# A Gram matrix from two fp16 words per value, and the same from fp32 products over 64 rows

## The reference, cut to what matters

```
nrm = jnp.maximum(jnp.sqrt(jnp.sum(xf * xf, axis=1)), EPS)
xn = xf / nrm[:, None, :]
s = jax.nn.relu(jnp.einsum('bcp,bcq->bpq', xn, xn)) ** GAMMA      # GAMMA = 2
g = jnp.einsum('oc,bcp->bop', Wc, xf) + bc[None, :, None]
out = jnp.einsum('bpq,bcq->bcp', s, g)
```

## Time and profile before

| | |
|---|---|
| median of 3 runs | 10261.85 us (10230.19 to 10309.07) |
| the profiled execution | 10185.96 us, its span 10184.3 us |
| granted TensorE clock, mean over the span | 0.697 |
| phase `images`, read from the trace | about 1,396 to 4,405 us |
| PE busy there, 1441 to 4403 us | 2845.77 of 2962.00 us |
| DVE, ACT busy there | 1613.24 us, 2116.29 us |

### The profile page before, as it was taken

One profiled execution on the slowest core, in us unless ns is written; L12 is line 12 of the kernel. 1 busy time (PEld: TensorE's weight loads), 2 busy tenths in 40 slices (PEclk: granted clock), 3 DMA queues, 4 the chain that ended last, 5 costly groups with the idle time before them and its releaser, 6 DMA issues. The chain is left out here.

```text
span 10184.3 us, 68577 instructions
## 1 busy us (share of the span) xinstructions
PE 4164.2 (41%) x19790; PEld 1375.6 (14%) x19790; DVE 4173.9 (41%) x4589; ACT 2803.9 (28%) x4023; POOL 3415.4 (34%) x3423
## 2 busy tenths in 40 slices
PE   0011049999999999930000000000000000388888
PEld 0011013333333333310000000000000000022222
DVE  8888965555555555521111111111121233333333
ACT  0000057777777777720000000000000000133322
POOL 2000000000000000047777777777777677300000
PEclk9755569999999999965555555555555555577777
DMA  0000001110111011111111111111111111111111
GB/s 8 0 0 0 16 11 29 31 28 27 29 29 31 27 29 29 31 23 17 19 23 17 19 21 19 17 23 19 17 23 17 15 11 11 31 43 43 43 43 33
DMA packets 244518, 230.15 MB, mean 23 GB/s; under 512 B 149261, under 2 KB 209400, under 8 KB 243448
## 3 DMA queue, kind: packets, MB, share of 16 engines
q1 hardware_dynamic: 122888, 166.61, 5.5%
q0 software_dynamic: 108864, 58.68, 4.6%
q10 hardware_dynamic: 12480, 1.18, 0.1%
HBM read 105.83 MB, written 101.55 MB: 20 GB/s over the span
## 5 line engine op out<-in xcount | busy, mean ns | idle before, releaser
L1197 POOL DMA_INDIRECT rows<-htab_d,idx x2624 | 2698.5, 1028 | 799.7 <-issue 799.7
L1041 DVE TENSOR_TENSOR s<-rel 128x1024 f32<-128x1024 f32 (+1 forms) x960 | 1070.6, 1117 | 1336.0 <-ACT rel L898 1336.0
L898 ACT ACTIVATE rel<-gram 128x1024 f32<-128x1024 f32 (+1 forms) x1440 | 1343.8, 940 | 723.7 <-PE gram L790 681.5
L1217 PE MATMUL tailsT<-ident,tails 128*20 128x128 f32 x24 | 5.0, 405 | 3536.7 <-DVE tails L1322 3536.7
L770 PE MATMUL acc<-s,gT 128*64 128x512 f32 (+1 forms) x5760 | 1435.0, 577 | 0.0
L1283 DVE TENSOR_TENSOR A<-rows,stg 128x328 f32<-128x328 f32 x32 | 30.5, 954 | 2917.3 <-DMA rows<-htab_d,idx 2917.3
L789 PE MATMUL gram<-hl 128*128 128x512 f16 (+1 forms) x2880 | 1033.4, 364 | 88.0 <-ACT rel L898 51.3
L790 PE MATMUL gram<-hl,lh 128*128 128x512 f16 (+1 forms) x2880 | 1020.3, 360 | 0.0
L1178 POOL IOTA offi<- 128x328 int32 x1 | 0.4, 402 | 3017.9 <-POOLq L512 3017.9
L1229 ACT ACTIVATE FX<-X 128x656 f32<-128x656 f32 x32 | 24.0, 749 | 3453.6 <-DVE X L1292 3453.6
L1702 DVE TENSOR_TENSOR hg<-gb,hid 128x384 f32<-128x384 f32 x768 | 394.2, 554 | 837.0 <-ACT hid L1664 667.5
(11 more groups left out here) (313 smaller groups left out, 4980.6 us busy)
## 6 DMA issues: line engine op xcount, KB each, us to landing
rows<-htab_d,idx POOLq DMA_INDIRECT x2624
seg_d<-rows SPq DMA_DIRECT2D x32, 984.0 KB, 3.9
lh<-hl SPq DMA_DIRECT2D x64, 288.0 KB, 3.7
x_d<-x SPq DMA_DIRECT2D x32, 576.0 KB, 3.2
tn_d<-tf SPq DMA_DIRECT2D x32, 576.0 KB, 2.8
tne<-tn_d SPq DMA_DIRECT2D x32, 576.0 KB
x2e<-x_d SPq DMA_DIRECT2D x32, 576.0 KB
xh<-in_x SPq DMA_DIRECT2D x66, 256.0 KB, 3.8
```

The lines of the kernel that those rows point to most:

```text
L898: act.activation(rel[:, t % RELS, 0:2 * w].rearrange("p (j x) -> p j x", j=2), gram[(par + t) % 2][:, :, 0:w], ACT.Relu, scale=1.0 / SPLIT ...
L1041: dve.tensor_tensor(s2[:, t % SLOTS, 0:2 * w], rel[:, t % RELS, 0:2 * w], rel[:, t % RELS, 0:2 * w], ALU.mult).then_inc(v_s2, 1)
L1197: pool.indirect_dma_start(out=rows[:, c % 2, j, :], out_offset=None, in_=n.htab, in_offset=bass.IndirectOffsetOnAxis(ap=idx[:, par, c * CW ...
```

## The change

The Gram blocks become fp32 products over 64 rows. `tw` is fp32 and holds `tk` twice, side by side (DVE writes it with two multiplications in `units`, L969 of the changed kernel). After the transposes rows 0 to 63 and rows 64 to 127 of `hl` (now fp32) hold the same unit columns. The block j = 0 is a product over rows 0 to 63, the block j = 1 one over rows 64 to 127, each into its own bank. `tk`, `high`, `low`, `lh`, `swap_halves`, `ident16` go. A PSUM bank holds four fp32 transposes, so there are five batches of four or fewer instead of three of eight; PE starts them two steps earlier.

```diff
-    TBATCH = [(q, min(8, QT - q)) for q in range(0, QT, 8)]
+    TBATCH = [(q, min(4, QT - q)) for q in range(0, QT, 4)]
...
-        tk = sb("tk", [P, QT, C])
-        tw = sb("tw", [P, QT, 2, C], F16)
-        hl = sb("hl", [P, 2, NP], F16)
-        lh = sb("lh", [P, 2, NP], F16)
+        tw = sb("tw", [P, QT, 2, C])
+        hl = sb("hl", [P, 2, NP])
...
-            def swap_halves(par):
-                sp.dma_start(lh[0:C, par, :], hl[C:P, par, :]).then_inc(l_in[par], 16)
-                sp.dma_start(lh[C:P, par, :], hl[0:C, par, :]).then_inc(l_in[par], 16)
...
                 if i == 0:
-                    pe.wait_ge(v_lo, b + 1)
+                    pe.wait_ge(v_t, b + 1)
...
-                pe.wait_ge(l_in[par], 32 * (nth + 1))
+                pe.wait_ge(a_hl, NTB * (b + 1))
...
-                        pe.matmul(bank[:, j, 0:w], hl[:, par, pixels], hl[:, par, o:o + w], start=True, stop=False)
-                        last = pe.matmul(bank[:, j, 0:w], lh[:, par, pixels], hl[:, par, o:o + w], start=False, stop=True)
+                        half_rows = slice(j * C, (j + 1) * C)
+                        last = pe.matmul(bank[:, j, 0:w], hl[half_rows, par, pixels], hl[half_rows, par, o:o + w], start=True, stop=True)
...
-                    if more and t == 33:
+                    if more and t == 31:
                         turn(b + 1, 0)
                         turn(b + 1, 1)
+                    if more and t == 33:
+                        turn(b + 1, 2)
+                        turn(b + 1, 3)
                     if more and t == 35:
-                        turn(b + 1, 2)
+                        turn(b + 1, 4)
...
-            def high(b):
-                act.wait_ge(v_t, b + 1)
-                at_least(act, pe_tr, NTB * b)
-                act.activation(tw[:, :, 0, :], tk[:, :, :], ACT.Copy).then_inc(a_hi, 1)
...
-                    if more and t == 30:
-                        high(b + 1)
-                    if more and t == 34:
+                    if more and t == 32:
                         turned(b + 1, 1 - par, 0)
                         turned(b + 1, 1 - par, 1)
+                    if more and t == 34:
+                        turned(b + 1, 1 - par, 2)
+                        turned(b + 1, 1 - par, 3)
                     if more and t == 36:
-                        turned(b + 1, 1 - par, 2)
+                        turned(b + 1, 1 - par, 4)
...
-                dve.tensor_tensor(tk[:, :, :], cv[:, :, 0:C], wide(scl[:, :]), ALU.mult).then_inc(v_t, 1)
+                at_least(dve, pe_tr, NTB * b)
+                for a in range(2):
+                    last = dve.tensor_tensor(tw[:, :, a, :], cv[:, :, 0:C], wide(scl[:, :]), ALU.mult)
+                last.then_inc(v_t, 1)
...
-            def low(b):
-                dve.wait_ge(a_hi, b + 1)
-                dve.tensor_tensor(tw[:, :, 1, :], tk[:, :, :], tw[:, :, 0, :], ALU.subtract).then_inc(v_lo, 1)
```

More of the change, by code:

```diff
@@ L560, in images @@
         epsc = sb("epsc", [P, 2])
-        ident16 = sb("ident16", [P, P], F16)
         gram = [pb(f"gram{i}", [P, 2, 512]) for i in range(2)]
@@ L579, in images @@
         v_t = sem("v_t")
-        a_hi = sem("a_hi")
-        v_lo = sem("v_lo")
         v_g = sem("v_g")
@@ L584, in images @@
         a_hl = sem("a_hl")
-        l_in = [sem("l_in0"), sem("l_in1")]
         pe_gram = sem("pe_gram")
@@ L666, in _ @@
             load(1, 1)
-            sp.wait_ge(a_hl, NTB)
-            swap_halves(0)
             def body(b, par, nth, before, more):
@@ L672, in body @@
                     tokens_out(b - 1)
-                if more:
-                    sp.wait_ge(a_hl, NTB * (b + 2))
-                    swap_halves(1 - par)
                 sp.wait_ge(v_x2, NCH * (b + 1))
@@ L692, in _ @@
             pool.tensor_tensor(centre[:, :], n.ident[0:C, 0:C], mean[:, :], ALU.subtract).then_inc(const_ready, 1)
-            pool.tensor_copy(ident16[:, :], n.ident[:, :]).then_inc(const_ready, 1)
             pool.memset(epsc[:, 0:1], 1e-6).then_inc(const_ready, 1)
@@ L698, in _ @@
         def _(pe):
-            pe.wait_ge(const_ready, 4)
+            pe.wait_ge(const_ready, 3)
             pe.wait_ge(w_in, 80)
@@ L724, in turn @@
                 if i == 0:
-                    pe.wait_ge(v_lo, b + 1)
+                    pe.wait_ge(v_t, b + 1)
                 if i >= 2:
                     pe.wait_ge(a_hl, NTB * b + i - 1)
-                bank = misc[:, i % 2, :].bitcast(F16)
+                bank = misc[:, i % 2, :]
                 for q in range(q0, q0 + k):
-                    last = pe.transpose(bank[:, (q - q0) * P:(q - q0 + 1) * P], tw[:, q, :, :].rearrange("p a c -> p (a c)"), ident16[:, :])
+                    last = pe.transpose(bank[:, (q - q0) * P:(q - q0 + 1) * P], tw[:, q, :, :].rearrange("p a c -> p (a c)"), n.ident[:, :])
                 last.then_inc(pe_tr, 1)
@@ L821, in _ @@
         def _(act):
-            act.wait_ge(const_ready, 4)
+            act.wait_ge(const_ready, 3)
             def pre(b, i):
@@ L856, in turned @@
                 act.wait_ge(pe_tr, NTB * b + i + 1)
-                act.activation(hl[:, par, q0 * P:(q0 + k) * P], misc[:, i % 2, :].bitcast(F16)[:, 0:k * P], ACT.Copy).then_inc(a_hl, 1)
+                act.activation(hl[:, par, q0 * P:(q0 + k) * P], misc[:, i % 2, 0:k * P], ACT.Copy).then_inc(a_hl, 1)
             def post(b, i):
@@ L885, in _ @@
             norm(0)
-            high(0)
             for i in range(NTB):
@@ L936, in _ @@
             dve.wait_ge(wct_ps, 1)
-            dve.wait_ge(const_ready, 4)
+            dve.wait_ge(const_ready, 3)
             dve.tensor_copy(wcT[:, :], misc[0:C, 0, 0:C]).then_inc(w_ready, 1)
@@ L1032, in _ @@
             units(0)
-            low(0)
             def body(b, par, nth, before, more):
@@ L1057, in body @@
                         units(b + 1)
-                    if more and t == 31:
-                        low(b + 1)
             walk(dve, body)
```

## The result

| | before | changed |
|---|---|---|
| median | 10251.76 us (4 runs, 10230.19 to 10309.07) | 10418.48 us (4 runs, 10375.58 to 10449.06) |
| span of the profiled execution | 10184.3 us | 10373.9 us |
| first `ssq` of `images` to the last (31 images) | 1420.1 to 4281.9: 2861.8 us | 1420.7 to 4436.8: 3016.1 us |
| one image that nothing disturbs | 91.52 us | 95.98 us |

The change makes the kernel slower by 1.5%; 1.7% were forecast.

The account below looks back on a forecast made before the run. PE's own queue, plus where PE stands, was taken to bound `images`; +137 (Gram products) + 34 (transposes) + 5 (stalls) - 4 (image 0) = +172 us on the median 10262 gave 10434, stated as 10430, range 10310 to 10510.

Parts of the forecast that it names:

- old stalls go (`high`, `low`): In each image, PE's waits for `rel` behind `high` (1.63 us) and for `low` (0.48) vanish, together 2.1 us.
- new stall comes (two passes into `tw`): Ahead of the transposes at step 31, PE stands 2.3 us for each image until DVE ends both passes of `units`.
- the forms without any stall: In each image, the added time of Gram products (0.095 us a step, 45 steps) and transposes (1.1 us), stalls aside.
- The Gram products: In each step of `images`, Gram start to `acc` start takes 1.06 us instead of 0.965; +137 us in all.
- Rival 2: In the Gram pairs, the second weight load is hidden, 0.107 us less a step; +41 us, 10303, not slower; chance 0.08.
- the prediction's sign of 0.93: In the changed trace, eight fp32 transposes should take 0.93 us up to the next Gram product.
- transposes of the next image: On PE's queue, 18 fp32 transposes cost 0.06 us more each, 1.1 us for each image, +34 us over 31 images.
- Rival 1: Ahead of the transposes, the new stall does not appear, DVE being early; 68 us less, +104 us, 10366; chance 0.12.
- Image 0: Preparation of the first image, without `swap_halves` waits and `high`: -4 us, between -7 and 0.
- Rival 4: In `images`, the clock falls to 1.2 GHz as often as in the experts; near 11400 us; chance 0.03.
- 137 + 34 + 5: Over `images`, the added us of the Gram products, of the transposes, and of the new stall less the old ones.
- Rival 3: In the Gram products, the two blocks don't run at once, 0.854 us more for 36 steps; near 11500 us; chance 0.04.

Follow-up runs that it names:

- e7: The kernel before with its split (`high`, `low`), transposes and their copies two steps later, single steps kept; 10026.95 us, ratio 0.9933 to the kernel before.
- e1: The changed kernel with its transposes and their copies two steps later; 10155.96 us, ratio 1.0054 to the kernel before.
- e5: The changed kernel with DVE's two passes into `tw` one step earlier, ahead of the value rows, transposes unmoved; 10156.36 us in one run.
- e3: e1 with PE's Gram products, then its value products, issued in groups of two steps; 9952.41 us, ratio 0.9877 to the kernel before.
- e2: The changed kernel with both Gram blocks of a step over rows 0 to 63, so they can't run at once; 11414.92 us in one run.
- e6: The kernel before with the later split of e7 and the groups of two steps of e4; 9920.52 us, ratio 0.9828 to the kernel before.
- e8: The changed kernel run again unaltered, on the chip of the other follow-up runs; 10241.85 us, ratio 1.0147 to the kernel before.
- e4: The kernel before with PE's work in groups of two steps, nothing moved; 10097.08 us, ratio 1.0007 to the kernel before.

## Why the prediction was right

The mechanism was right: more time in the Gram products, and a new stall for two old ones. The size was near in part by luck, as below. For an undisturbed image:

| | predicted | measured | from |
|---|---|---|---|
| old stalls go (`high`, `low`) | -2.1 | -2.24 | before less e7 |
| new stall comes (two passes into `tw`) | +2.3 | +2.33 | changed less e1 |
| the forms without any stall | +5.4 | +4.37 | e1 less e7 |
| together | +5.6 | +4.46 | |

(The three measured rows add up to the last by the way they are taken; that is no test of them. The tests are the waits that went in e1, e5 and e7.)

- **The Gram products**: +0.095 us a step, from `up` in another phase, was right to 0.01: it measures +0.092. The place of it was read rightly too, as the load records of e3 show: the second weight load starts 0.107 us late. Per weight column that is 0.83 ns, and the 0.05 us of `acc` with 64 columns fit it. What the prediction lacked is the condition: this is so behind a change of shape alone. Rival 2 (load hidden) is out for the single steps, and right inside e3's groups. The Trainium skill (TensorE: Matmul & The Clock Gate, Part 3, "The mechanism") has weight loads pulled ahead of products in flight, and packed tiles that take the time of one product plus about 4 ns for each further one. The record pairs behind an equal shape, 0.43 apart with the partner 7 ns later, agree with it, and the first one behind another shape, 0.53, does not. Why no load is pulled ahead over a change of shape no run shows.
- **The term that was mis-sized** is the neighbours. I priced each Gram product as if it always stood behind `acc`. Behind `pre` and `post`, which have the new form's own shape (64 rows), it now costs less. Timeline of PE, changed kernel:

```profile
2551.56 1.16 PE L701 MATMUL misc<-wpre,xh 64*128 64x128 f32 x16
2552.55 1.03 PE L774 MATMUL gram<-hl 64*128 64x512 f32 x4
2553.51 1.08 PE L754 MATMUL acc<-s,gT 128*64 128x512 f32 x4
```

  Gram to `acc` is 0.96 us there and not 1.06 (0.99 behind `post`), and the batch ahead ends 0.10 us sooner too, at three places each. Against that, fp32 transposes ahead of a Gram product now meet a change of shape that wasn't there: 1.02 us instead of 0.93 for eight (the prediction's sign of 0.93 failed).

```profile
2587.47 1.09 PE L714 MATMUL misc<-ident,tw 128*128 128x128 f32 x8
2588.49 1.13 PE L774 MATMUL gram<-hl 64*128 64x512 f32 x4
```

  The distances between the starts on PE in one undisturbed image, e1 less e7, account for the third row of the table:

  | | predicted | measured |
  |---|---|---|
  | 45 Gram products | +4.3 | +3.68 |
  | transposes of the next image | +1.1 | +1.38 |
  | `pre` and `post`, six batches | 0 | -0.59 |
  | `tokens`, two batches | 0 | +0.19 |
  | `acc`, with PE's waits ahead of `post` and `tokens` | 0 | -0.28 |
  | together | +5.4 | +4.38 |

- **What the old stalls paid for the new one** was right: they cancel, 2.24 against 2.33, and the reading that DVE's chain hangs on an early Gram product gave the 2.26 us of the trace to 0.04. (The sum has +5 us where 0.2 x 31 are 6; nothing rests on it.) Rival 1 is out for the change as it is, and is what e1 and e5 are.
- **Image 0**: the first Gram product starts at 1433.88 instead of 1437.73, -3.9; -4 was taken.
- **Not foreseen**: 15 more short stretches at 1.2 GHz, some 1.6 us each, +24 us, though the prediction had the clock at full throughout. Rival 4 had the clock falling for whole stretches because of the form; it fell for moments, in 14 places right behind the new stall, and without that stall (e1, e5) in none of these. From `ssq` to `ssq` the 154 us are: -3 in the first interval (image 0, whose preparation is shorter), 30 x 4.54 = +136 for the other images (by the sums of the preparation, where the kernel before has 91.44), +24 for the clock, and an estimated -3 at the 14 turns of the loop, the remainder.
- **Luck**: the whole phase, from the first Gram product to the last `acc`, grew by 166 us where 137 + 34 + 5 = 176 were forecast. The image was priced 1.1 us too high, 35 us in all, and the 24 us of the clock were left out. The two errors have nothing to do with each other and happen to offset.
- **Rival 3** is out: e2 shows what it would have been.

## What to carry to other kernels

Two fp32 products over 64 rows at once replace two fp16-split products over 128 rows at nearly the same price; what is left of the difference goes with how often the array changes its shape, since here each change costs about 0.10 us and lays the next fp32 weight load bare, 0.107 more for 128 columns. In single steps the fp32 form is 4.4 us an image behind, in groups of two (e3 against e6) 1.5. Group work of one shape, and look at what stands next to a product before pricing it. An operation that makes one engine wait for another inside a loop of steps (here `high`, or the passes into `tw`) belongs two steps later, where its input is long done: that alone was worth 0.7% for the fp16 form here (e7) and 0.9% for the fp32 form (e1 against e8), and grouping the fp16 form without it was worth nothing (e4).

## What was not expected of the hardware

- With both blocks on the lower half of the rows, PE busy without a gap was granted 1.2 GHz for up to 116 us at a time, and 2.4 GHz in stretches as long with the same work (e2, one run), while the form that fills both halves held 2.4 GHz but for short stretches. The experts before showed the like, 1.2 GHz with PE busy for 92% of 41 us.
- Stands of PE in a stream of products were followed by a short stretch at 1.2 GHz or not, in one and the same code: those of 3.37 us (e4) in 30 of 31 places, those of 2.26 (changed) in 14 of 31, those of 1.6 (before) in none of 31, and those of some 2 us at the turns of the loop in 9 of 14 (changed), 12 of 14 (e1) and 2 of 14 (e7).
- The same gather of 2,624 indirect DMAs took 2693 to 2699 us of busy time in nine executions and 2831 in one.
